# Graph layer on one core: layer 2 on split operands with 512 moving columns, its output turned back, and rings of six

## Chip, core and metric

One Trainium2 chip, one of its cores. The metric is the device time of one execution in microseconds; a comparison takes the median of several executions. The kernel before ran three times: 213.15 us median, 213.1 to 213.64.

## What is computed

`x` is 6250 nodes by 128, `edge_attr` is 106250 edges by 128, and `dst` (sorted) names the node of each edge. All in f32.

```python
h   = relu(layernorm(x))
agg = segment_sum(edge_attr, dst, 6250)          # [6250, 128]
hid = relu(concatenate([agg, h], axis=1) @ W1 + b1)   # W1 [256, 512]
out = x + hid @ W2 + b2                          # W2 [512, 128]
```

## The kernel before

Nodes are taken in NB = 25 blocks of 256 (the last has 106), edges in 69 full rounds of 1536 and a rest round. A round is one transfer of 768 KB into one slot of the ring `edges` (RING = 8 slots). VectorE (`build`, L474 to 486) compares the edges' relative node numbers with an iota and writes a one-hot matrix per round into a ring of HOTS = 8. TensorE (`sum_rounds`, L776) multiplies one-hot by edges, two, three or four rounds per block, into bank 0; ScalarE copies the sums out (`copy_sums`), TensorE turns them (`turn_sums`), and VectorE adds each piece of 32 nodes at its place in `aggT` (`add_sums`, L565), at addresses that `load_bases` reads into its registers.

Beside this runs the layer norm of block b: `stats` on VectorE, `spread` on Pool (four small instructions), `normalise` on ScalarE, `turn_x` on TensorE, `h_out` on ScalarE and `rest_of_h` on VectorE. The last two split the turned block in a high part `hT_hi` of type f32r and the rest `hT_lo`. `round_agg` and `rest_of_agg` do the same to the sums.

The network runs on groups: blocks 0, 1 and 2 alone, then pairs of blocks (3,4), (5,6) up to (23,24), so NS = 14 groups of which ten have 512 columns and the last 362. Layer 1 (`layer1_h` L828, `layer1_agg` L837) makes three f32r products for each of four parts t of 128 hidden units, the group's columns moving. `relu` on ScalarE (L409) writes `hidden` in f32, one instruction a part. `layer2` (L854) has `hidden` as weights and W2 as moving operand, in plain f32 with 128 moving columns: eight instructions for a single block, 16 for a pair. Its result has nodes on the partitions, so `finish` on VectorE adds it straight to `x`, to which `add_b2` (L507) has added b2, and SyncE stores it.

The order on each engine is written out by hand, as one loop over k = 1 to 24. Blocks up to k = 3 (EARLY) have an order of their own. From k = 5 on, an odd k holds layer 1 of a pair, the even k after it its layer 2:

```python
                    sum_rounds(k)
                    if k == EARLY + 1:
                        turn_x(k)
                    if two is not None:
                        layer2(two, two)
                    if one is not None:
                        layer1_h(one, one)
                    turn_sums(k)
                    if k + 1 < NB:
                        turn_x(k + 1)
                    if one is not None:
                        layer1_agg(one, one, blocks_of(one)[-1] + 1)
```

All loads and stores go out on SyncE's queue in order; `load(r)` waits until round r - RING has been summed. Semaphores are waited for in program order, so an instruction that waits holds all behind it on its engine.

## Time and profile before

| | us |
|---|---|
| median of three executions | 213.15 |
| the profiled execution, whole | 212.71 |
| its span in the trace | 210.5 |
| TensorE busy in the span | 193.7 |
| VectorE busy | 131.5 |
| ScalarE busy | 84.7 |
| Pool busy | 43.0 |

The profiled execution took 2.21 us more than its span (what lies outside the first and last instruction), and 0.44 us less than the median. Busy time of TensorE counts overlapping matmuls once. A plain f32 matmul shows as two records in the trace, so the 200 instructions of `layer2` are 400 records; an f32 transpose and an f32r matmul are one record each.

### The profile page before, as it was taken

Reading aid. Unit: us, or ns where it says so; the run is one execution under the profiler, and the core shown is the slowest. Engines: PE = TensorE matmul, PEld = TensorE weight load, DVE = VectorE, ACT = ScalarE, POOL = GpSimd, SP = SyncE. Lnnn points to the kernel's source line nnn. Section 1 sums busy time; section 2 is a strip of 40 time slices with the busy share of each in tenths; the row PEclk is TensorE's granted clock in tenths of the full one; section 3 lists DMA queues with packets and bytes.
Section 4 is the critical chain, followed back from the end, with each engine's and each line's share of the span. In section 5 each row is a group of like instructions: output and inputs, shape, how many; then the busy total and the mean of one; then the engine's idle time right before and its main releaser. Section 6 shows DMA issues by size and latency. Waiting matters only on the chain.

```text
span 210.5 us, 6775 instructions
## 1 busy us (share of the span) xinstructions
PE 193.7 (92%) x2549; PEld 164.9 (78%) x2549; DVE 131.5 (62%) x581; ACT 84.7 (40%) x185; POOL 43.0 (20%) x120
## 2 busy tenths in 40 slices
PE   1397999998999999999999999999999999999990
PEld 1165878788789888798898897887986987978990
DVE  1945754729766967786768579676774775853300
ACT  3031354272482363543713814734436236136030
POOL 5554020220222012202220221122022022200000
PEclk9999999999999999999999999999999999999997
DMA  6899999999999999999999999999999780010101
GB/s 213 272 391 361 377 371 377 376 375 385 386 377 384 377 376 387 377 380 384 365 350 372 328 381 376 311 299 386 306 379 378 226 320 36 3 50 3 50 15 30
DMA packets 44623, 62.55 MB, mean 297 GB/s; under 512 B 1795, under 2 KB 44294, under 8 KB 44588
## 3 DMA queue, kind: packets, MB, share of 16 engines
q1 hardware_dynamic: 44116, 61.66, 83.4%
q10 hardware_dynamic: 472, 0.43, 0.8%
q8 instruction: 22, 0.36, 0.7%
q14 instruction: 13, 0.11, 0.1%
HBM read 58.88 MB, written 3.20 MB: 295 GB/s over the span
## 4 chain that ended last, share of the span: by engine, by line
PE 79%; DMA 11%; SPq 3%; DVE 2%; ACT 1%; issue 1%; DVEq 0%; ACTq 0%
PE bank L854 21%; PE bank L793 20%; PE bank L828 16%; PE bank L837 15%; DMA edges<-in_edge_attr 6%; DMA xs<-in_x 5%; PE bank L804 3%; SPq L257 3%; PE bank L814 2%; PE bank L786 1%; ACT xn L378 1%; DVE aggT L576 1%; SPq L282 0%; ACT sums L393 0%; SPq L280 0%
## 5 line engine op out<-in xcount | busy, mean ns | idle before, releaser
L793 PE MATMUL bank<-edges,onehot 128*32 128x128 f32 x1656 | 55.1, 285 | 4.7 <-DMA edges<-in_edge_attr 3.9
L793 PEld LDWEIGHTS bank<-edges,onehot 128*32 128x32 f32 x1656 | 45.3, 114 | 12.5 <-issue 5.6
L854 PE MATMUL bank<-w,hidden 128*128 128x128 f32 (+1 forms) x400 | 48.5, 278 | 0.4 <-DVE outrow L552 0.4
L409 ACT ACTIVATE hidden<-bank,b_col 128x512 f32<-128x512 f32 (+2 forms) x56 | 34.2, 633 | 35.3 <-PE bank L837 35.3
L854 PEld LDWEIGHTS bank<-w,hidden 128*128 128x128 f32 (+1 forms) x400 | 45.8, 189 | 3.1 <-issue 2.2
L576 DVE TENSOR_TENSOR aggT<-bank,aggT 128x32 f32 x277 | 35.3, 190 | 17.0 <-issue 10.9
L378 ACT ACTIVATE xn<-xs,shift,rstd 128x128 f32<-128x128 f32 (+1 forms) x50 | 21.7, 484 | 44.4 <-POOL shift L334 44.2
L327 POOL TENSOR_SCALAR var<-meanvar 128x2 f32<-128x2 f32 (+1 forms) x25 | 7.3, 293 | 133.1 <-DVE meanvar L504 133.0
L484 DVE TENSOR_TENSOR onehot<-relT,iota 128x384 f32<-128x384 f32 x69 | 34.4, 552 | 0.0
L828 PE MATMUL bank<-hT_hi,w_hi 128*128 128x512 f32 (+2 forms) x56 | 22.5, 402 | 0.0
L837 PE MATMUL bank<-agg_hi,w_hi 128*128 128x512 f32 (+2 forms) x56 | 21.4, 382 | 0.3 <-DVE agg_lo L526 0.3
L828 PE MATMUL bank<-hT_lo,w_hi 128*128 128x512 f32 (+2 forms) x56 | 20.9, 372 | 0.0
L828 PE MATMUL bank<-hT_hi,w_lo 128*128 128x512 f32 (+2 forms) x56 | 20.7, 370 | 0.0
L837 PE MATMUL bank<-agg_hi,w_lo 128*128 128x512 f32 (+2 forms) x56 | 20.4, 364 | 0.0
L837 PE MATMUL bank<-agg_lo,w_hi 128*128 128x512 f32 (+2 forms) x56 | 20.3, 363 | 0.0
L332 POOL TENSOR_TENSOR rstd<-var,power 128x2 f32<-128x2 f32 (+1 forms) x25 | 17.7, 708 | 2.1
L399 ACT ACTIVATE agg_hi<-aggT 128x256 fp32r<-128x256 f32 (+1 forms) x25 | 10.7, 428 | 18.0 <-DVE aggT L576 17.9
L520 DVE TENSOR_TENSOR hT_lo<-bank,hT_hi 128x256 fp32r<-128x256 f32 (+1 forms) x25 | 10.3, 414 | 11.5 <-ACT hT_hi L385 11.4
L526 DVE TENSOR_TENSOR agg_lo<-aggT,agg_hi 128x256 fp32r<-128x256 f32 (+1 forms) x25 | 10.5, 419 | 8.8 <-ACT agg_hi L399 8.8
L499 DVE BATCH_NORM_STATS2 halves<-xs 128x6 f32<-128x128 f32 (+1 forms) x50 | 12.0, 281 | 5.5 <-DMA xs<-in_x 5.5
L393 ACT ACTIVATE sums<-bank 128x384 f32<-128x384 f32 (+3 forms) x25 | 11.7, 466 | 7.0 <-PE bank L793 6.1
L828 PEld LDWEIGHTS bank<-hT_hi,w_hi 128*128 128x128 f32 x56 | 10.9, 194 | 4.2 <-issue 2.8
(94 smaller groups left out, 170.8 us busy)
## 6 DMA issues: line engine op xcount, KB each, us to landing
edges<-in_edge_attr SPq DMA_DIRECT2D x69, 768.0 KB, 9.3
xs<-in_x SPq DMA_DIRECT2D x21, 128.0 KB, 9.3
out_rows<-outrow SPq DMA_DIRECT2D x10, 256.0 KB
w<-in_L_gnn_W SPq DMA_DIRECT2D x1, 512.0 KB, 9.7
out_rows<-outrow SPq DMA_DIRECT2D x4, 128.0 KB, 8.4
xs<-in_x SPq DMA_DIRECT2D x1, 256.0 KB, 11.4
w<-in_L_gnn_W SPq DMA_DIRECT2D x1, 256.0 KB, 12.8
hidden<-in_dst SPq DMA_DIRECT2D x1, 192.0 KB, 3.1
```

The source lines that it names most:

```text
L332: nc.gpsimd.tensor_tensor(rstd[0:w, par, :], var[0:w, par, :], power[0:w, :], ALU.pow).then_inc(pow_ready, 1)
L378: ins = nc.scalar.activation(xn[0:w, par, j, :], xs[0:w, b, j * F:(j + 1) * F], ACT.Relu, bias=shift[0:w, par, j:j + 1], scale=rstd[0:w, p ...
L393: nc.scalar.activation(sums[0:rows, k % 2, 0:n], sums_ps[0:rows, 0:n], ACT.Copy).then_inc(sums_copied, 1)
L399: nc.scalar.activation(agg_hi[:, halves].rearrange("f (j p) -> f j p", j=2), aggT[:, bass.ds(b * BLOCK, halves.stop - halves.start)].rearr ...
L409: nc.scalar.activation(hidden[:, t, 0:cols], hid_ps[t][:, 0:cols], ACT.Relu, bias=b1_col[:, t:t + 1]).then_inc(hidden_ready, 1)
L484: nc.vector.tensor_tensor(hot, of.unsqueeze(2).to_broadcast([p, n, W]), iota[0:p, 0:W].unsqueeze(1).to_broadcast([p, n, W]), ALU.is_equal) ...
L499: nc.vector.bn_stats(halves[0:w, par, j, :], xs[0:w, b, j * F:(j + 1) * F]).then_inc(halves_ready, 1)
L576: nc.vector.tensor_tensor(win, turn_ps[:, at:at + W], win, ALU.add).then_inc(agg_added, 1)
L793: ins = nc.tensor.matmul(sums_ps[t * W:(t + 1) * W, cols], onehot[:, hots, e, :], edges[:, slot, e * F:(e + 1) * F], start=(g == 0), stop= ...
L828: nc.tensor.matmul(hid_ps[t][:, 0:cols], wt[:, 1, to], v[:, here], start=(i == 0), stop=False)
L837: ins = nc.tensor.matmul(hid_ps[t][:, 0:cols], wt[:, 0, to], v[:, 0:cols], start=False, stop=(i == 2))
L854: ins = nc.tensor.matmul(o[0:w, j * F:(j + 1) * F], hidden[:, t, at:at + w], w2[:, t, :], start=(t == 0), stop=(t == HT - 1))
```

## The change

Layer 2 is turned round. Its weights are now the parts of W2, split as `w2_hi` and `w2_lo` of type f32r (made once, at k = 1: ScalarE L506, VectorE L761); the moving operand is the hidden part with all columns of the group, split as `hid_hi` and `hid_lo`. That is three f32r matmuls for each of four parts. The result has features on the partitions: ScalarE copies it out with b2 as bias (`out_copy`, L480), TensorE turns it back into the same bank (`turn_out`, L983), and `finish` reads that. `add_b2` is left only for the last two blocks; the last group keeps the old form (`layer2_last`).

To have `hid_lo`, ScalarE runs two instructions a part, one that writes the f32 value `full` (in the buffer of `w1`, two parts deep) and one that writes `hid_hi`. Pool subtracts for parts 0 and 1, VectorE for parts 2 and 3. ScalarE waits for `lo_by_pool` before it writes parts 2 and 3 into `full`. The rings of edges and one-hots have six slots. `dst` lands in the sixth edge slot, so the sixth load waits until `dst` has been read. The loads of `x` stand earlier in SyncE's order, and the stats, spread and normalise steps of two blocks stand together in every second k.

```diff
-RING = 8
-HOTS = 8
+RING = 6
+HOTS = 6
@@ Pool
-            for b in range(1, NB):
-                spread(b)
+            def rest_of_hidden(n, s):
+                cols = cols_of(s)
+                for t in range(HALF):
+                    pool.wait_ge(hidden_ready, n * HT + t + 1)
+                    nc.gpsimd.tensor_tensor(hid_lo[:, t, 0:cols], full[:, t % 2, 0:cols],
+                                            hid_hi[:, t, 0:cols].bitcast(F32), ALU.subtract).then_inc(lo_by_pool, 1)
...
+            for k in range(EARLY + 2, NB, 2):
+                for b in (k + 3, k + 4):
+                    if b < NB:
+                        spread(b)
+                rest_of_hidden(group1(k), group1(k))
@@ ScalarE, relu and what is new
-                    nc.scalar.activation(hidden[:, t, 0:cols], hid_ps[t][:, 0:cols], ACT.Relu,
-                                         bias=b1_col[:, t:t + 1]).then_inc(hidden_ready, 1)
+                    if t >= HALF:
+                        act.wait_ge(lo_by_pool, split_before(n) * HALF + t - HALF + 1)
+                    elif not (isinstance(n, int) and n == 0):
+                        act.wait_ge(lo_by_dve, (split_before(n) - 1) * HALF + t + 1)
+                    nc.scalar.activation(full[:, t % 2, 0:cols], hid_ps[t][:, 0:cols], ACT.Relu, bias=bias_col[:, t:t + 1])
+                    nc.scalar.activation(hid_hi[:, t, 0:cols], hid_ps[t][:, 0:cols], ACT.Relu,
+                                         bias=bias_col[:, t:t + 1]).then_inc(hidden_ready, 1)
+
+            def out_copy(n, s):
+                cols = cols_of(s)
+                act.wait_ge(out_summed, n + 1)
+                nc.scalar.activation(outT[:, 0:cols], out_ps[:, 0:cols], ACT.Identity,
+                                     bias=bias_col[:, HT:HT + 1]).then_inc(outT_ready, 1)
@@ VectorE
+            def rest_of_hidden(n, s, t):
+                cols = cols_of(s)
+                dve.wait_ge(hidden_ready, n * HT + t + 1)
+                nc.vector.tensor_tensor(hid_lo[:, t, 0:cols], full[:, t % 2, 0:cols], hid_hi[:, t, 0:cols].bitcast(F32),
+                                        ALU.subtract).then_inc(lo_by_dve, 1)
@@ TensorE
+            def layer2(n, s, first=0, last=HT):
...
+                for t in range(first, last):
+                    if t < HALF:
+                        pe.wait_ge(lo_by_pool, split_before(n) * HALF + t + 1)
+                    else:
+                        pe.wait_ge(lo_by_dve, split_before(n) * HALF + t - HALF + 1)
+                    products = ((w2_hi, hid_hi), (w2_hi, hid_lo), (w2_lo, hid_hi))
+                    for i, (wt, v) in enumerate(products):
+                        ins = nc.tensor.matmul(out_ps[:, 0:cols], wt[:, t, :], v[:, t, 0:cols], start=(t == 0 and i == 0),
+                                               stop=(t == HT - 1 and i == 2))
...
+            def turn_out(n, s):
+                pe.wait_ge(outT_ready, split_before(n) + 1)
+                for j in range(cols_of(s) // P):
+                    ins = nc.tensor.transpose(out_ps[:, j * F:(j + 1) * F], outT[:, j * P:(j + 1) * P], ident[:, :])
+                ins.then_inc(out_turned, 1)
@@ TensorE, the loop from k = 4 on
+                elif one is not None:
+                    sum_rounds(k)
+                    turn_out(group3(k), group3(k))
+                    layer1_h(one, one)
+                    turn_sums(k)
+                    if k + 1 < NB:
+                        turn_x(k + 1)
+                    layer1_agg(one, one, blocks_of(one)[-1] + 1)
                 else:
                     sum_rounds(k)
...
+                    layer2(two, two, 0, 3)
                     turn_sums(k)
+                    layer2(two, two, 3)
                     if k + 1 < NB:
                         turn_x(k + 1)
```

How the instructions now stand, in rows of the program's order. First TensorE at k = 6 and the start of k = 7 (`bank` is a PSUM bank, `w` and `hidden` are W2 and the hidden units). Before:

```order
L793 MATMUL bank<-edges,onehot 32x128 x36
L854 MATMUL bank<-w,hidden 128x128 x16
L804 MATMUL bank<-ident,sums 128x128 x3
L814 MATMUL bank<-ident,xn 128x128 x2
L793 MATMUL bank<-edges,onehot 32x128 x36
L828 MATMUL bank<-hT_hi,w_hi 128x512
```

After, from the last of the first three parts on:

```order
L975 MATMUL bank<-hid_hi,w_hi 128x512
L975 MATMUL bank<-hid_lo,w_hi 128x512
L975 MATMUL bank<-hid_hi,w_lo 128x512
L928 MATMUL bank<-ident,sums 128x128 x3
L975 MATMUL bank<-hid_hi,w_hi 128x512
L975 MATMUL bank<-hid_lo,w_hi 128x512
L975 MATMUL bank<-hid_hi,w_lo 128x512
L938 MATMUL bank<-ident,xn 128x128 x2
L917 MATMUL bank<-edges,onehot 32x128 x36
L983 MATMUL bank<-ident,outT 128x128 x4
L952 MATMUL bank<-hT_hi,w_hi 128x512
```

Sixteen instructions have become twelve with four times the columns, turning the sums (L928) stands between the third and the fourth part, and four transposes (L983) stand ahead of the next layer 1.

Second ScalarE at k = 1, behind the first group's sums. Before:

```order
L399 ACTIVATE agg_hi<-aggT 128x256
L409 ACTIVATE hidden<-bank,b_col 128x256 x4
L378 ACTIVATE xn<-xs,shift,rstd 128x128 x2
L393 ACTIVATE sums<-bank 128x384
L378 ACTIVATE xn<-xs,shift,rstd 128x128 x2
L385 ACTIVATE hT_hi<-bank 128x256
```

After, from the last of four pairs of relu instructions on (`w` at L473 is `full`, in the buffer of w1; at L506 it is W2):

```order
L473 ACTIVATE w<-bank,bias_col 128x256
L474 ACTIVATE hid_hi<-bank,bias_col 128x256
L506 ACTIVATE w_hi<-w 128x512
L434 ACTIVATE xn<-xs,shift,rstd 128x128 x2
L449 ACTIVATE sums<-bank 128x384
L434 ACTIVATE xn<-xs,shift,rstd 128x128 x2
L441 ACTIVATE hT_hi<-bank 128x256
```

Eight relu instructions and the rounding of W2 now stand ahead of the normalising of block 1 and of the copy of the sums, where four relu instructions stood.

## Rows read from the trace of the kernel before

**Rows 1.** The page: busy tenths in 40 slices of 5.26 us.

```profile
PE   1397999998999999999999999999999999999990
DMA  6899999999999999999999999999999780010101
```

**Rows 2.** The chain that ended last: start us, us, what; two stretches.

```profile
56.55 3.02 PE bank L837 x12
...
169.15 2.10 PE bank L793 x72
171.25 3.00 PE bank L828 x12
174.25 0.33 PE bank L804 x3
174.57 0.22 PE bank L814 x2
174.79 2.77 PE bank L837 x12
177.56 1.45 PE bank L793 x48
179.01 3.77 PE bank L854 x32
```

**Rows 3.** ScalarE and VectorE by line and form: count, busy us, mean ns, idle before.

```profile
L409 ACT ACTIVATE hidden<-bank,b_col 128x512 f32<-128x512 f32 x40 | 27.4, 688 | 27.0 <-PE bank L837 26.9
L484 DVE TENSOR_TENSOR onehot<-relT,iota 128x384 f32<-128x384 f32 x69 | 34.4, 552 | 0.0
L554 DVE TENSOR_TENSOR outrow<-bank,xs 128x512 f32<-128x512 f32 x10 | 6.9, 692 | 10.8 <-DMA out_rows<-outrow 4.6 <-issue 2.5 <-PE bank L854 2.4
```

**Rows 4.** Timeline of ScalarE: start us, us, instruction; relu of block 0, then of a pair.

```profile
24.94 1.57 ACT L409 ACTIVATE hidden<-bank,b_col 128x256 f32<-128x256 f32 x4 [1.45 <-PE bank L837]
26.38 0.89 ACT L378 ACTIVATE xn<-xs,shift,rstd 128x128 f32<-128x128 f32 x2
...
175.53 2.76 ACT L409 ACTIVATE hidden<-bank,b_col 128x512 f32<-128x512 f32 x4 [2.95 <-PE bank L837]
178.19 0.87 ACT L378 ACTIVATE xn<-xs,shift,rstd 128x128 f32<-128x128 f32 x2
```

**Rows 5.** Timeline of TensorE, 27 to 46 us, with the idle time before.

```profile
27.34 0.44 PE L814 MATMUL bank<-ident,xn 128*128 128x128 f32 x2
...
29.30 2.05 PE L854 MATMUL bank<-w,hidden 128*128 128x128 f32 x16
...
36.59 0.55 PE L804 MATMUL bank<-ident,sums 128*128 128x128 f32 x3 [0.24 <-ACT sums L393]
...
45.58 0.55 PE L804 MATMUL bank<-ident,sums 128*128 128x128 f32 x3 [0.24 <-ACT sums L393]
```

**Rows 6.** Timelines of VectorE and ScalarE, 43 to 48 us.

```profile
43.38 0.25 DVE L504 BATCH_NORM_AGGREGATE meanvar<-halves 128x2 f32<-128x6 f32 x2
...
45.43 1.64 ACT L378 ACTIVATE xn<-xs,shift,rstd 128x128 f32<-128x128 f32 x4
...
47.36 0.42 DVE L520 TENSOR_TENSOR hT_lo<-bank,hT_hi 128x256 fp32r<-128x256 f32 x1 [2.50 <-ACT hT_hi L385]
```

**Rows 7.** Pool by line and form: count, busy us, mean ns, idle before.

```profile
L350 POOL MEMSET aggT<- 128x832 f32 x8 | 6.0, 791 | 1.4 <-DVE relA L581 1.4
L334 POOL TENSOR_TENSOR shift<-negmean,rstd 128x2 f32<-128x2 f32 x24 | 4.7, 195 | 1.9
```

**Rows 8.** Timelines of Pool and VectorE: L327 of block 1 and of a later block.

```profile
18.35 0.22 POOL L327 TENSOR_SCALAR var<-meanvar 128x2 f32<-128x2 f32 x1 [4.48 <-DVE meanvar L504]
...
101.65 0.30 POOL L327 TENSOR_SCALAR var<-meanvar 128x2 f32<-128x2 f32 x1 [5.72 <-DVE meanvar L504]
...
101.48 0.39 DVE L513 TENSOR_TENSOR xs<-xs,b_all 128x256 f32<-128x256 f32 x1
```

**Rows 9.** The page: DMA issues, count, KB each, median us to landing.

```profile
edges<-in_edge_attr SPq DMA_DIRECT2D x69, 768.0 KB, 9.3
```

More of the change, by code:

```diff
@@ L298, in _ @@
                         load(r + RING)
[L299 to L300 removed]
+                if not early and group3(k - 1) is not None:
+                    store(group3(k - 1), group3(k - 1))
             store(NS - 2, NS - 2)
@@ L439, in _ @@
                     copy_sums(k)
                     normalise(k + 1)
-                if k == EARLY:
-                    normalise(k + 2)
-                if not early and k + 2 < NB:
-                    normalise(k + 2)
+                    if k == EARLY:
+                        normalise(k + 2)
+                elif one is not None:
+                    h_out(k)
+                    copy_sums(k)
+                    round_agg(k - 1, chunks_by(k - 1), place(k - 1), group_of(k - 1))
+                    if k + 1 < NB:
+                        h_out(k + 1)
+                    relu(one, one)
+                else:
+                    if k == EARLY + 1:
+                        h_out(k - 1)
+                    copy_sums(k)
+                    if k == EARLY + 1:
+                        h_out(k)
+                    round_agg(k - 1, chunks_by(k - 1), place(k - 1), group_of(k - 1))
+                    out_copy(two, two)
+                    for b in (k + 2, k + 3):
+                        if b < NB:
+                            normalise(b)
@@ L457, in again_group @@
                     relu(n, s)
+                    if not (isinstance(s, int) and s == NS - 1):
+                        out_copy(n, s)
                 for s in range(ONES):
@@ L653, in _ @@
                         build(r)
-                rest_of_agg(k - 1, k - 1, place(k - 1))
+                if k == EARLY + 1 or (k > EARLY and one is None):
+                    rest_of_h(k)
+                if k <= EARLY:
+                    rest_of_agg(k - 1, k - 1, place(k - 1))
                 if k + 1 < NB:
@@ L698, in _ @@
                     nc.vector.tensor_scalar(flag[:, :], colD[:, 6:7], 0.0, None, ALU.is_gt).then_inc(flag_ready, 1)
+                if k > EARLY and one is None:
+                    rest_of_agg(k - 1, k - 1, place(k - 1))
                 bases = load_bases(k)
-                if group2(k) is not None:
-                    finish(group2(k), group2(k))
+                if k <= EARLY and group3(k) is not None:
+                    finish(group3(k), group3(k))
             add_sums(NB - 1, bases)
             rest_of_agg(NB - 1, NB - 1, place(NB - 1))
+            finish(NS - 2, NS - 2)
+            add_b2(NB - 2)
             add_b2(NB - 1)
```

206 lines of the change are left out of this document (138 added, 68 removed).

## The prediction

> **What bounds the kernel now.** I read the page's slices first, then the chain, then the timelines of the engines that feed TensorE. The slices show TensorE at nine tenths nearly throughout, and a DMA that is as full until slice 31 and then falls off while TensorE goes on [rows 1]. So the transfers finish early, and the end is set by TensorE. The chain says the same: from 56.55 us on it is TensorE's own instructions one behind the other, with no idle piece between them [rows 2]. There every microsecond taken from or added to TensorE's stream counts in full, and so does every wait. Before that the chain passes through other engines: TensorE waits for sums and layer norms that ScalarE and VectorE hand over [rows 5, 6]. The question is thus what twelve wide products save on TensorE, and whether ScalarE, Pool and VectorE deliver split hidden parts in time.
>
> **TensorE's own work.** A pair of blocks (odd k, then even k) costs, by the chain, 2.10 + 3.00 + 0.33 + 0.22 + 2.77 for the odd k and 2.10 + 3.77 + 0.33 + 0.22 for the even one, 14.84 us together; three of the ten even k have two rounds, 1.45 in place of 2.10 [rows 2]. Layer 2 is the 3.77. The new one has twelve f32r products with 512 moving columns, like layer 1. Nine come behind the rounds, as L828 does (9/12 of 3.00, 2.25), three behind transposes, as L837 (3/12 of 2.77, 0.69). Four f32 transposes at 0.11 each (0.33 for three, [rows 2]) are 0.44, and splitting the products around the turning of the sums gives one more change of kind, about 0.1 (the 3.00 against the 2.77 shows what one costs, at most 0.23). The sum is 3.48 against 3.77: **0.29 less a pair, 2.9 less for ten**. The bounds are 0.1 and 0.5 a pair. The last group is unchanged. Single blocks gain some 0.3 each, which is in the steps below.
>
> **The start, k = 1 to 5.** One relu of 256 columns takes a pitch of 0.36 (26.38 less 24.94, over four [rows 4]), and there are now eight. At k = 1 relu starts at 24.94 as before and ends at 27.8; rounding W2 (512 columns, one pitch of a pair's relu, 0.59) ends at 28.4; only then block 1 is normalised, 0.8, to 29.2. TensorE wanted it at 27.34 [rows 5]. The sums are copied behind it in some 0.5 (384 columns, between the pitches 0.36 for 256 and 0.59 for 512) and turned at 29.7; before, with both done in time, the turning was 0.7 behind L814's 27.34, so it is 1.7 late. At k = 2 layer 2 costs 1.5 in place of 2.05 [rows 5], so layer 1 ends 1.1 late; relu then holds ScalarE for 2.9 and not 1.4, the copy of the sums stands behind it, and the turning at 36.59 goes to 38.6. At k = 3 the same: layer 2 waits a little for `finish` of block 0, which on VectorE now stands behind two subtractions, and 45.58 becomes 48.05, 2.5 late. At k = 4 there is a second chain. VectorE takes the stats of block 5 behind the subtractions of group 2, so they end at 48.75, not at 43.63; Pool needs 1.75 for the spread (before, from 43.63 to the normalising at 45.43 [rows 6]), ScalarE 0.8 for block 5's normalising and 0.35 for `h_out`, so VectorE's `rest_of_h` (47.36, [rows 6]) starts at 51.7, 4.3 late. At k = 5 VectorE has also the subtraction of `finish` and the stats of block 7 ahead of what layer 1 of the first pair needs, and I get that start at 61.3 where the chain has 56.55 [rows 2]: **4.8 more**. Bounds: 2, if only the first delay stays, and 6.5.
>
> **A pair's hidden parts.** Let A be the start of `layer1_agg` in the chain, 174.79. Relu starts at 175.53, A + 0.74 [rows 2, 4]. Its four instructions last 2.76, each 0.69 [rows 3], so the last starts at 177.60, and the next instruction at 178.19: a pitch of 0.59 where nothing is waited for. Parts 0 to 3 are then high at A + 2.0, 3.2, 4.4 and 5.6. TensorE reaches parts 0 and 2 at A + 4.87 and A + 6.4, the turning of the sums at A + 7.1 and part 3 at A + 7.45; all 0.65 earlier with two rounds. VectorE's subtraction of 512 columns I take at 0.69, as L554 [rows 3]: part 3 is ready at A + 6.3. That would be 1.1 in hand, but Pool lies between: relu may not begin part 2 before Pool's part 0 is done. Pool's subtraction is not in the trace. Below, it lies at 0.49 + 0.2: one stream of 832 columns takes 0.79 [rows 7], so 512 take 0.49, and the same kind on two columns takes 0.195. Above, three streams of 0.49 and 0.2, 1.7. I take two streams, as its two inputs seem the nearer count to a write-only memset: **1.2 us**. (The Trainium skill, GPSIMD Engine Reference, section 3.1, has 2.6 cycles an element for this kind at 1.2 GHz, which makes 1.1; no run here has yet shown it.) Pool also has two spreads of 1.45 to 1.75 ahead of it, whose stats VectorE ends near A. So its part 0 ends about A + 3.8, part 1 at 5.0, and relu's part 3 is high at 6.2, its rest ready at 7.0, still in hand by 0.4 with three rounds, and late by 0.2 with two.
>
> Then VectorE. It loses one `add_b2` a block (0.39) and gains two subtractions a pair (1.3), so it is about 0.5 busier, and in the first pair, still late from the start, its stats come so late that Pool begins part 0 at about A + 5: TensorE waits 0.9 there. VectorE builds one-hots (0.55, [rows 3]) just while Pool works. Pool's L327 on the same two columns takes 0.22 at block 1 and 0.30 at a later block, where VectorE's two-input L513 runs until 0.22 after its start [rows 8]; the two may hold each other up. (The Trainium skill, SBUF — State Buffer, section "SBUF: two separate sides", calls their shared port pair an exclusive lock against two-input VectorE instructions; the 0.08 agrees, and is all the trace has of it.) For what a few such meetings and the pairs with two rounds cost I take 0.25 for each of nine pairs, 2.2; below it is 0, above it is 1.2, one whole Pool instruction.
>
> **Ring and loads.** With six slots a load is issued when the round six before it is summed, two blocks ahead, some 13 us, and lands 9.3 after issue [rows 9]. I cost it at nothing; if that cover went, TensorE would wait for edges. Moving b2 into `out_copy`, the extra small load, the earlier loads of x and the later sixth load stand beside other work: nothing. `out_copy` and `turn_out` have the rounds of the next k between them.
>
> **Sum.** 4.8 - 2.9 + 0.9 + 2.2 = 5.0 us more. The profiled execution had 212.71, the median 213.15; on the median that is **218.2**, and I say 218.0.
>
> **Rivals.**
> - *ScalarE and Pool stay covered and the start heals.* TensorE's idle at the start is partly made up, since VectorE's and Pool's queues are shorter than I reckon and x comes earlier; no pair waits. From the point where the start costs less than 2.6 us the change is faster. With a start at +1 it is 213.15 - 2.9 + 1 = 211.3. For it: the hidden parts are in hand by 0.4 on paper. Against: the first 1.7 at k = 1 follows from ScalarE's order alone. 0.14.
> - *Pool and VectorE block each other in every pair.* If one-hots wait for a Pool subtraction and Pool for one-hots, part 3 comes about 1 us late ten times: 213.15 + 4.8 - 2.9 + 10 = 225.2. For it: the 0.30 against 0.22, and the rule of the page named above, which by the same working gives this 225. Against: 0.08 is little. 0.2.
> - *The ring starves.* If transfers bunch and land 15 us after issue, TensorE waits about 1.5 a pair: 213.15 + 2 + 15, some 230. Against: TensorE takes its 4.98 MB a pair more slowly than the DMA has brought them so far. 0.04.
> - *Forecast*, 213.3 to 222, 0.62.
>
> **The numbers.** Differences under 0.3% (0.64 us) can't be told here. Faster: the first rival, less its near part, 0.12. Same: its edge and the forecast's lower edge, 0.05. Slower: 0.83. The range takes the lower bounds of start and waits (213.15 + 2 - 2.9 + 1 = 213.3) and upward most of the second rival: 213.3 to 224.0; what is left out is most of the first rival and the upper part of the second and third.
>
> **What would show it.** Right: L975 and L983 together about 3.4 a pair on TensorE; TensorE idle at L938 near 29 us, and at the turning of the sums at k = 2 and 3 for ScalarE; the first pair's `layer1_agg` (L961) near 61; Pool's L389 near 1.2; waits at L975 for VectorE's rest. Wrong: a first pair near 57, or Pool's L389 stretched beyond 1.7, or TensorE waiting for edges.

## The result and the profile after

| | before | after |
|---|---|---|
| median of four executions, us | 213.39 | 229.69 |
| lowest to highest | 213.1 to 214.07 | 228.85 to 231.23 |
| the profiled execution, whole | 212.71 | 231.23 |
| its span | 210.5 | 229.4 |

The change makes the kernel slower by 7.9% (ratio 1.079, interval 1.075 to 1.084). The forecast was 218.0, range 213.3 to 224.0: the sign is right, the size is not (16.3 us more, not 5). The profiled execution is the slowest of its four, so the pieces below add up to its own 18.9 us of span; 1.5 us of them lie between it and the median. Here and below, medians and ratios leave out executions in the chip's slower state, in which the granted clock is lower and the time over 1.5% above the kernel's fastest.

The page of the changed kernel, first the busy times, then the slices (5.74 us each) and the chain by engine and by line:

```profile
PE 196.4 (86%) x2383; PEld 155.2 (68%) x2383; DVE 149.7 (65%) x587; ACT 117.7 (51%) x251; POOL 73.4 (32%) x146
...
PE   1498688775999998989999779989999879999990
...
PEclk9999979999799999999999999999999999999998
DMA  6899999897897989989969979989799499200011
...
PE 40%; DMA 23%; DVE 20%; issue 6%; ACT 4%; SPq 2%; POOL 2%; DVEq 1%; ACTq 0%; POOLq 0%
DMA out_rows<-outrow 19%; PE bank L917 11%; PE bank L961 9%; PE bank L952 7%; DVE onehot L571 7%; PE bank L975 6%; DMA edges<-in_edge_attr 4%; DVE aggT L671 3%; DVE halves L586 2%; PE bank L998 2%; SPq L282 2%; DVE outrow L643 2%; ACT hid_hi L474 1%; DVE hid_lo L650 1%; PE bank L928 1%
```

Two things stand out beside [rows 1]. TensorE has holes from slice 4 to 10, the start, and then again and again to the end. And the chain, which was TensorE's own [rows 2], now lies for 19% in a **store**: `out_rows<-outrow`. No term of the prediction had a store in it.

The starts of `layer1_agg` (L837 before, L961 after) cut the span into stretches that can be compared. They are the first record of that line for the group:

| | first pair (3,4) | tenth pair (21,22) | the nine steps between | from there to the end |
|---|---|---|---|---|
| before | 56.52 | 188.83 | 132.31 | 21.7 |
| after | 65.08 | 207.75 | 142.67 | 21.7 |
| difference | +8.6 | | +10.4 | 0.0 |

The start was predicted at +4.8 and the pairs at 0.9 + 2.2 less 2.9, about nothing. So the start took almost twice what was forecast, and the pairs took ten microseconds that the forecast did not have.

**Where TensorE waits.** The waits of the changed kernel, those of TensorE alone (total us, times, longest us):

```profile
PE bank L975 <- DVE hid_lo L650: 4.5, 7, 1.6
...
PE bank L928 <- ACT sums L449: 3.4, 3, 1.3
PE bank L975 <- POOL hid_lo L389: 2.7, 6, 0.6
PE bank L961 <- DVE agg_lo L612: 2.5, 3, 1.4
PE bank L938 <- DVE hT_lo L606: 2.2, 1, 2.2
PE bank L938 <- ACT xn L434: 2.2, 1, 2.2
PE bank L975 <- DVE outrow L641: 0.6, 1, 0.6
```

The rows for `hid_lo` are the pairs', and so is 1.9 of the 2.5 us for `agg_lo` (9.1 us together); the others are the start's. The idle time that a row shows is less than what is lost, since ends of matmuls are modelled. One pair shows it. Timeline of TensorE in the changed kernel, layer 2 of the pair (7,8), from the last product of its first part to the start of its third:

```profile
101.75 0.40 PE L975 MATMUL bank<-hid_hi,w_lo 128*128 128x512 f32 x1
102.67 0.50 PE L975 MATMUL bank<-hid_hi,w_hi 128*128 128x512 f32 x1 [0.52 <-POOL hid_lo L389]
103.01 0.40 PE L975 MATMUL bank<-hid_lo,w_hi 128*128 128x512 f32 x1
103.24 0.40 PE L975 MATMUL bank<-hid_hi,w_lo 128*128 128x512 f32 x1
104.15 0.50 PE L975 MATMUL bank<-hid_hi,w_hi 128*128 128x512 f32 x1 [0.51 <-DVE hid_lo L650]
```

Products that follow one another start 0.23 us apart (103.01 to 103.24). Across the wait the starts are 0.92 apart, so 0.69 is lost where the row says 0.52. With TensorE's saving of 0.39 a pair (measured below), the nine steps hold 10.4 + 3.5, some 14 us of waits.

**The store.** Timeline of the changed kernel around the pair (9,10), SyncE first, then VectorE, TensorE and Pool:

```profile
115.89 2.31 SPq L282 DMA_DIRECT2D edges<-in_edge_attr  x3
118.25 0.51 SPq L300 DMA_DIRECT2D out_rows<-outrow  x1
...
109.24 0.68 DVE L643 TENSOR_TENSOR outrow<-bank,xs 128x512 f32<-128x512 f32 x1
...
123.86 0.42 DVE L606 TENSOR_TENSOR hT_lo<-bank,hT_hi 128x256 fp32r<-128x256 f32 x1
127.24 0.69 DVE L643 TENSOR_TENSOR outrow<-bank,xs 128x512 f32<-128x512 f32 x1 [2.96 <-DMA out_rows<-outrow]
127.84 0.42 DVE L612 TENSOR_TENSOR agg_lo<-aggT,agg_hi 128x256 fp32r<-128x256 f32 x1
...
128.31 0.50 PE L961 MATMUL bank<-agg_hi,w_hi 128*128 128x512 f32 x1 [1.35 <-DVE agg_lo L612]
...
129.09 0.22 POOL L354 TENSOR_SCALAR var<-meanvar 128x2 f32<-128x2 f32 x1 [11.90 <-DVE meanvar L591]
```

And the chain of waits there (start us, us, what):

```profile
117.70 0.50 SPq L282
118.25 8.90 DMA out_rows<-outrow
127.24 0.69 DVE outrow L643
...
128.31 3.06 PE bank L961 x12
```

`finish` (L643) writes `outrow` at 109.24. The store of it stands on SyncE behind the loads of the even k, which wait for their slots, so it is issued only at 118.25, 8.3 us after `finish` ended, and is done 8.9 us later. The next `finish` was ready to go at 124.28 and waits 2.96 for it, since for pairs there is one `outrow`. Behind it in VectorE's queue stand `agg_lo`, for which TensorE waits, and the stats of two blocks, for which Pool waits, which has then its spreads ahead of its subtractions. In the kernel before the order was another: `finish` stood at the end of the even k, behind `agg_lo` and the stats. Its store stood behind the loads of the odd k that follows at once, and in the corresponding place it was issued 1.8 us after `finish` ended (111.37 to 113.13). `finish` waited for stores there too, 4.6 us in all [rows 3], but no wait of TensorE in the pairs came of it.

**Pool and VectorE hold each other up.** By line and form, the changed kernel (count, busy us, mean ns, idle before):

```profile
L571 DVE TENSOR_TENSOR onehot<-relT,iota 128x384 f32<-128x384 f32 x69 | 45.2, 706 | 0.0
...
L389 POOL TENSOR_TENSOR hid_lo<-w,hid_hi 128x512 fp32r<-128x512 f32 x20 | 27.6, 1402 | 12.8 <-ACT hid_hi L474 12.8
...
L643 DVE TENSOR_TENSOR outrow<-bank,xs 128x512 f32<-128x512 f32 x10 | 6.9, 691 | 11.3 <-DMA out_rows<-outrow 7.8 <-PE bank L983 2.0 <-issue 1.6
```

The same one-hot instruction took 552 ns before [rows 3] and now takes 706 on average (544 to 1645). Timelines of Pool and VectorE in one pair:

```profile
99.77 2.84 POOL L389 TENSOR_TENSOR hid_lo<-w,hid_hi 128x512 fp32r<-128x512 f32 x2
...
100.65 2.85 DVE L571 TENSOR_TENSOR onehot<-relT,iota 128x384 f32<-128x384 f32 x3
```

Three one-hots, 1.49 us when alone (at 99.33 in the kernel before), take 2.85 beside Pool's two subtractions. VectorE's own subtractions stand behind them.

**The start.** Timeline of TensorE in the changed kernel: its longest waits from k = 1 to 4, and the two rounds that follow:

```profile
29.52 0.69 PE L938 MATMUL bank<-ident,xn 128*128 128x128 f32 x2 [2.17 <-ACT xn L434]
...
40.78 0.55 PE L928 MATMUL bank<-ident,sums 128*128 128x128 f32 x3 [1.34 <-ACT sums L449]
...
50.91 0.55 PE L928 MATMUL bank<-ident,sums 128*128 128x128 f32 x3 [1.34 <-ACT sums L449]
...
55.14 0.41 PE L938 MATMUL bank<-ident,xn 128*128 128x128 f32 x2 [2.24 <-DVE hT_lo L606]
...
58.68 2.92 PE L917 MATMUL bank<-edges,onehot 128*32 128x128 f32 x72
```

The places are the ones forecast. The first turning of the sums is nearly where it was reckoned (30.0 against 29.7), the next two are later: 40.78 and 50.91 against 38.6 and 48.05. The last row is a loss of another kind: 72 records that take 2.17 at full clock (experiment 12) take 2.92, in one of the two slices where the page's granted clock falls to 7 tenths; the other holds the wait at 29.52. Windows of this trace put the granted clock at 0.51 from 30.0 to 33.0 and at 0.50 from 57.0 to 60.0, about the lower of its two levels (1.2 of 2.4 GHz). Six microseconds at half the clock are about 3 us of delay (an estimate from these windows), and the kernel before has no such slice.

### The profile page after: what moved, and what is told of

Read it like the earlier page. It is cut to its first block, busy times and chain, and to the rows that moved or that the text cites. A ratio compares the mean times of both kernels' runs of the same rounds, so it can differ in the third digit from the quotient of the medians.

```text
span 229.4 us, 6586 instructions
## 1 busy us (share of the span) xinstructions
PE 196.4 (86%) x2383; PEld 155.2 (68%) x2383; DVE 149.7 (65%) x587; ACT 117.7 (51%) x251; POOL 73.4 (32%) x146
## 4 chain that ended last, share of the span: by engine, by line
PE 40%; DMA 23%; DVE 20%; issue 6%; ACT 4%; SPq 2%; POOL 2%; DVEq 1%; ACTq 0%; POOLq 0%
DMA out_rows<-outrow 19%; PE bank L917 11%; PE bank L961 9%; PE bank L952 7%; DVE onehot L571 7%; PE bank L975 6%; DMA edges<-in_edge_attr 4%; DVE aggT L671 3%; DVE halves L586 2%; PE bank L998 2%; SPq L282 2%; DVE outrow L643 2%; ACT hid_hi L474 1%; DVE hid_lo L650 1%; PE bank L928 1%
## 5 line engine op out<-in xcount | busy, mean ns | idle before, releaser
L473 ACT ACTIVATE w<-bank,bias_col 128x512 f32<-128x512 f32 (+1 forms) x52 | 33.3, 640 | 24.0 <-POOL hid_lo L389 12.2
L571 DVE TENSOR_TENSOR onehot<-relT,iota 128x384 f32<-128x384 f32 x69 | 45.2, 706 | 0.0
L389 POOL TENSOR_TENSOR hid_lo<-w,hid_hi 128x512 fp32r<-128x512 f32 (+1 forms) x26 | 32.0, 1247 | 28.4 <-ACT hid_hi L474 28.4
L474 ACT ACTIVATE hid_hi<-bank,bias_col 128x512 fp32r<-128x512 f32 (+1 forms) x52 | 33.1, 636 | 0.0
L975 PE MATMUL bank<-hid_hi,w_hi 128*128 128x512 f32 (+1 forms) x52 | 23.2, 447 | 8.1 <-DVE hid_lo L650 4.5
L441 ACT ACTIVATE hT_hi<-bank 128x256 fp32r<-128x256 f32 (+1 forms) x25 | 9.3, 371 | 31.8 <-PE bank L938 31.8
L650 DVE TENSOR_TENSOR hid_lo<-w,hid_hi 128x512 fp32r<-128x512 f32 (+1 forms) x26 | 15.5, 622 | 14.5 <-ACT hid_hi L474 14.5
L961 PE MATMUL bank<-agg_hi,w_hi 128*128 128x512 f32 (+2 forms) x56 | 21.6, 385 | 2.5 <-DVE agg_lo L612 2.5
L975 PEld LDWEIGHTS bank<-hid_hi,w_hi 128*128 128x128 f32 x52 | 10.1, 193 | 17.1 <-DVE hid_lo L650 8.6
L961 PE MATMUL bank<-agg_hi,w_lo 128*128 128x512 f32 (+2 forms) x56 | 20.4, 364 | 0.0
L961 PE MATMUL bank<-agg_lo,w_hi 128*128 128x512 f32 (+2 forms) x56 | 20.4, 364 | 0.0
L975 PE MATMUL bank<-hid_lo,w_hi 128*128 128x512 f32 (+1 forms) x52 | 19.4, 372 | 0.0
L975 PE MATMUL bank<-hid_hi,w_lo 128*128 128x512 f32 (+1 forms) x52 | 19.3, 372 | 0.0
```

The lines of the kernel that those rows point to most:

```text
L389: nc.gpsimd.tensor_tensor(hid_lo[:, t, 0:cols], full[:, t % 2, 0:cols], hid_hi[:, t, 0:cols].bitcast(F32), ALU.subtract).then_inc(lo_by_po ...
L473: nc.scalar.activation(full[:, t % 2, 0:cols], hid_ps[t][:, 0:cols], ACT.Relu, bias=bias_col[:, t:t + 1])
L474: nc.scalar.activation(hid_hi[:, t, 0:cols], hid_ps[t][:, 0:cols], ACT.Relu, bias=bias_col[:, t:t + 1]).then_inc(hidden_ready, 1)
L571: nc.vector.tensor_tensor(hot, of.unsqueeze(2).to_broadcast([p, n, W]), iota[0:p, 0:W].unsqueeze(1).to_broadcast([p, n, W]), ALU.is_equal) ...
L650: nc.vector.tensor_tensor(hid_lo[:, t, 0:cols], full[:, t % 2, 0:cols], hid_hi[:, t, 0:cols].bitcast(F32), ALU.subtract).then_inc(lo_by_dv ...
L961: ins = nc.tensor.matmul(hid_ps[t][:, 0:cols], wt[:, 0, to], v[:, 0:cols], start=False, stop=(i == 2))
```

## Experiments

The theory after reading: of the 16 us, the store wait ahead of `agg_lo` and the stats costs the most in the pairs, the mutual blocking the next, and the start is ScalarE's and VectorE's order. The rival: the rests are late because Pool and ScalarE are simply too slow for a pair (12.2 us of ScalarE's waits for Pool), so that order changes little. Each ratio is to the kernel before on the same chip. The chips differ: the kernel before has medians from 212.49 to 213.39 on them, so a difference between two experiments is good to about 1 us.

**1. Rings of six in the kernel before.**

```diff
-RING = 8
-HOTS = 8
+RING = 6
+HOTS = 6
```

> The kernel before with both rings cut from eight to six slots and nothing else. Theory W (the loss comes from waits in the chain relu, rests, store and finish): 213.4 us as before, within 0.6, TensorE waits for edges only at the start. Rival R (the smaller ring starves TensorE): most of the 16 us, at least 217.

Measured: 213.11 us, ratio 1.000 (0.998 to 1.002). The smaller rings cost nothing in the order of before, as the prediction had it; in the new order the ring of eight was not run.

**2. `finish` behind `agg_lo` and the stats** (odd k, VectorE).

```diff
-                    finish(group3(k), group3(k))
                     rest_of_agg(k - 1, k - 1, place(k - 1))
                     for b in (k + 3, k + 4):
                         if b < NB:
                             stats(b)
+                    finish(group3(k), group3(k))
```

> The changed kernel, but at odd k VectorE rounds off the sums (agg_lo) and takes the stats before it does finish. Theory S (finish waits for the store of the group before, 8.5 us after its issue, and holds all behind it on VectorE): VectorE still waits at finish, but TensorE no longer waits at layer1_agg, and Pool's spreads and its first subtraction come earlier in the pairs where ScalarE waited 2 us; 222 to 226 us. Rival (the store wait is mostly beside TensorE's work, which shows only 2 us idle at layer1_agg): 227 to 228.

Measured: 223.88 us, ratio 1.052 (1.049 to 1.055), 5.8 less than the change. `finish` itself now waits less as well; the row by form of this kernel:

```profile
L643 DVE TENSOR_TENSOR outrow<-bank,xs 128x512 f32<-128x512 f32 x10 | 6.8, 680 | 4.1 <-DMA out_rows<-outrow 2.8 <-PE bank L983 1.3
```

TensorE has no row left that waits for Pool's `hid_lo`, though nothing of Pool's work was changed: Pool had been late because the stats ahead of its spreads were. The move takes two things out of the way, the wait for the store and the instruction itself (0.69). Over the nine steps of the profiled executions it gives 6.9 us, of which 2.7 lie in steps where `finish` had waited 0.2 or less for a store. How the gain divides between the two is not shown by this run; 4 and 5 show it without the subtractions.

**3. One-hots behind VectorE's subtractions** (even k from 6 on), so that Pool and VectorE do not read side by side.

```diff
-                if k + 1 < NB:
+                late = k > EARLY + 1 and one is None
+                if k + 1 < NB and not late:
                     for r in ROUNDS[k + 1]:
                         build(r)
...
                         rest_of_hidden(group2(k), group2(k), 2)
                         rest_of_hidden(group2(k), group2(k), 3)
+                if k + 1 < NB and late:
+                    for r in ROUNDS[k + 1]:
+                        build(r)
```

> The changed kernel, but at even k from 6 on VectorE builds the next one-hots after its two subtractions, so they no longer run beside Pool's. Theory L (a Pool subtraction and a two-input VectorE instruction hold each other up): Pool's subtraction of 512 columns falls from 1.40 to 1.2 us or less, the one-hots from 0.71 to 0.55, and the time to about 225. Rival (Pool just takes 1.4 us, and one-hots are late for another reason): both durations stay and the time is within 1 us of 229.7, or longer, since the one-hots come later.

Measured: 227.66 us, ratio 1.069 (1.067 to 1.072), 2.0 less than the change. By form:

```profile
L571 DVE TENSOR_TENSOR onehot<-relT,iota 128x384 f32<-128x384 f32 x69 | 34.4, 551 | 0.0
...
L389 POOL TENSOR_TENSOR hid_lo<-w,hid_hi 128x512 fp32r<-128x512 f32 x20 | 25.2, 1282 | 11.7 <-ACT hid_hi L474 11.6
```

Both are back at a length of their own: the one-hot at 551 ns (552 before), Pool's subtraction at 1.28, a little above the 1.2 expected. So they do hold each other up. The gain is 2 us, less than the 4.7 expected and far from the 10 of the second rival; it is a net figure, since the one-hots now also come later.

**4. No rests at all.** `hid_lo` is a constant, nobody subtracts, and ScalarE runs one instruction a part.

```diff
-                    nc.scalar.activation(full[:, t % 2, 0:cols], hid_ps[t][:, 0:cols], ACT.Relu, bias=bias_col[:, t:t + 1])
...
-                for t in range(HALF):
+                for t in range(0):
                     pool.wait_ge(hidden_ready, n * HT + t + 1)
...
             def rest_of_hidden(n, s, t):
-                cols = cols_of(s)
-                dve.wait_ge(hidden_ready, n * HT + t + 1)
...
+                return
```

> The changed kernel without the rest of the hidden part: ScalarE writes only the high part (one instruction a part), hid_lo is filled once with a constant and read as before, Pool and VectorE subtract nothing. TensorE's instructions are the same. Left out: the correction of the hidden part's rounding. If TensorE's own saving is 0.29 us a pair and the loss is all in making the rests: 210 to 213 us. If the new order or the wide products cost TensorE by themselves: 215 or more.

Measured: 213.76 and 216.0 us (and 219.96 and 220.53 at a granted clock of 0.98), too far apart for a ratio. The profiled one (216.0, span 214.1) starts its first pair at 55.50, a little earlier than before does, and is slower than before all the same. By the expectation's numbers that would mean that the new order or the wide products cost TensorE something; the rows show that it is the order, by way of the store. The row for `finish` by form, two of its instructions in VectorE's timeline, and the row of TensorE's waits:

```profile
L640 DVE TENSOR_TENSOR outrow<-bank,xs 128x512 f32<-128x512 f32 x10 | 6.9, 692 | 24.0 <-DMA out_rows<-outrow 22.0 <-PE bank L974 2.0
```

```profile
70.84 0.69 DVE L640 TENSOR_TENSOR outrow<-bank,xs 128x512 f32<-128x512 f32 x1 [3.94 <-DMA out_rows<-outrow]
...
99.84 0.69 DVE L640 TENSOR_TENSOR outrow<-bank,xs 128x512 f32<-128x512 f32 x1 [1.06 <-DMA out_rows<-outrow]
```

```profile
PE bank L955 <- DVE agg_lo L609: 7.1, 6, 2.0
```

With every rest gone, VectorE stands 22.0 us before the stores and TensorE 7.1 us behind it. A VectorE with less to do only comes to the store earlier.

**5. No rests, and `finish` late** (4 and 2 together): what the change gives TensorE when nothing else is late.

```diff
-                    finish(group3(k), group3(k))
                     rest_of_agg(k - 1, k - 1, place(k - 1))
...
+                    finish(group3(k), group3(k))
```

> No rests are made (as in a_no_rest; left out is the correction of the hidden part's rounding), and finish stands behind agg_lo. Nothing but the start should then hold TensorE up, so it shows what TensorE's new instructions save alone. Theory: 0.29 a pair less than before, the pair 14.55 us from layer1_agg to layer1_agg where before has 14.82, and 209 to 211 us in all. Rival (the new instructions save nothing): pair at 14.8 and time at 213.

Measured: 207.09 us, ratio 0.975 (0.973 to 0.976). Over the nine steps the profiled execution is 8.6 us shorter than that of 4 (128.67 against 137.29).

Step by step, 4 and 5 separate the store wait from the instruction. In 4 `finish` stands ahead of `agg_lo` in every pair. Where it waits 1.06 or 0.66 us for a store, or not at all, the step is as long as in 5: the instruction in front costs nothing there. Where it waits 2.63 to 4.19, six times, the step is longer than in 5 by 0.69 to 2.28, each time by the wait less 1.9. So the whole 8.6 us are store waits, each beyond what lay covered. In 5 `finish` still waits 9.2 us for stores, and no pair is longer for it.

A pair of three rounds each takes 14.43 from one `layer1_agg` to the next, against 14.82 to 14.84 before (the first 14.44 and 14.88). TensorE's saving is thus **0.39 to 0.40 a pair**; the prediction had 0.29, within bounds of 0.1 and 0.5. Ten pairs make 4.0 of the 5.4 us; nearly all the rest, 1.3, is the single blocks', since the first pair starts at 55.19 and not at 56.52.

**6. Both moves with the rests in place** (2 and 3).

```diff
-                    finish(group3(k), group3(k))
                     rest_of_agg(k - 1, k - 1, place(k - 1))
...
+                    finish(group3(k), group3(k))
...
+                if k + 1 < NB and late:
+                    for r in ROUNDS[k + 1]:
+                        build(r)
```

> Both edits together: finish behind agg_lo and the stats at odd k, one-hots behind the two subtractions at even k. If store wait and blocking are two causes, their gains (5.8 and 2.0 us in the first four runs) add up to about 222; if they are one wait seen twice, it stays at 223.9.

Measured: 222.48 us, ratio 1.045 (1.042 to 1.049). Behind `finish` late, the later one-hots give 1.4 where they gave 2.0 alone. The two gains nearly add up, as for two causes; whether the missing 0.6 had been the same time can't be told, since the interval of each ratio is about 0.7 us to either side.

**7. The start in another order, on top of 6.** ScalarE at k = 1 rounds W2 and normalises block 1 ahead of the relu; for k up to 3 it copies the sums between relu parts 1 and 2; VectorE takes the stats, `w2_lo` and `finish` ahead of its subtractions; Pool spreads block 5 ahead of the rests of group 2.

```diff
@@ ScalarE
                 if k <= EARLY:
+                    if k == 1:
+                        act.wait_ge(w2_landed, 16)
+                        nc.scalar.activation(w2_hi[:, :, :], w2[:, :, :], ACT.Copy).then_inc(w2_hi_ready, 1)
+                        normalise(1)
...
-                    relu(one, one)
...
+                    relu(one, one, 0, HALF)
                     copy_sums(k)
+                    relu(one, one, HALF, HT)
@@ VectorE
                 if k <= EARLY:
-                    rest_of_hidden(one, one, 2)
-                    rest_of_hidden(one, one, 3)
                     stats(k + 2)
...
+                    if group3(k) is not None:
+                        finish(group3(k), group3(k))
+                    rest_of_hidden(one, one, 2)
+                    rest_of_hidden(one, one, 3)
```

> a_both_late, and the start reordered: at k = 1 ScalarE rounds W2 and normalises block 1 ahead of relu; at k = 1 to 3 it copies the sums between parts 1 and 2 of relu; VectorE takes the stats and finish ahead of its two subtractions; Pool's spread of block 5 stands ahead of group 2's. If the start's 8.6 us are these four orders, the first pair's layer1_agg comes at 58 to 60 instead of 65, and the time is 5 to 7 us under a_both_late. If the start is lost to the added work whatever its order, less than 2 us.

Measured: 217.63 us, ratio 1.026 (1.023 to 1.030), 4.9 less than 6 on the same chip (4.1 by the ratios). The first pair starts at 58.53, where 6 has 63.96. The largest wait left is at k = 4, for block 4's rest on VectorE; and in every pair ScalarE still waits for Pool. Timelines of TensorE and of ScalarE:

```profile
50.09 0.41 PE L943 MATMUL bank<-ident,xn 128*128 128x128 f32 x2 [2.97 <-DVE hT_lo L607]
...
108.96 0.69 ACT L473 ACTIVATE w<-bank,bias_col 128x512 f32<-128x512 f32 x1 [1.36 <-POOL hid_lo L389]
```

**8. All four subtractions on VectorE**, `finish` late, Pool free.

```diff
@@ Pool
-                for t in range(HALF):
+                for t in range(0):
@@ VectorE, rest_of_hidden(n, s, t)
+                first = 0 if t == 2 else 3
+                for u in range(first, t + 1):
+                    dve.wait_ge(hidden_ready, n * HT + u + 1)
+                    nc.vector.tensor_tensor(hid_lo[:, u, 0:cols], full[:, u % 2, 0:cols],
+                                            hid_hi[:, u, 0:cols].bitcast(F32),
+                                            ALU.subtract).then_inc(lo_by_dve if u >= HALF else lo_by_pool, 1)
```

> a_finish_late with all four subtractions on VectorE, Pool only spreads. No Pool instruction can block VectorE, but VectorE has 1.4 us more a pair, and relu's part 2 waits for VectorE's part 0, behind sums and one-hots. If blocking outweighs the work: under 223.9. If VectorE's added work counts: 226 or more.

Measured: 234.41 us, ratio 1.104 (1.102 to 1.107), some 11 more than with Pool (2). Waits of this kernel:

```profile
ACT w L473 <- DVE hid_lo L652: 25.4, 9, 6.2
...
PE bank L978 <- DVE hid_lo L652: 14.7, 17, 3.6
```

A VectorE subtraction takes 0.69 where Pool's takes 1.28, and still the kernel is slower: on VectorE the first parts stand behind one-hots and sums, and ScalarE waits up to 6.2 us for a free `full`. In this order Pool as a second engine is worth having; another order for the four subtractions on VectorE was not tried.

**9. Pool's rests between its two spreads**, on top of 7.

```diff
-                for b in (k + 3, k + 4):
-                    if b < NB:
-                        spread(b)
+                if k + 3 < NB:
+                    spread(k + 3)
                 rest_of_hidden(group1(k), group1(k))
+                if k + 4 < NB:
+                    spread(k + 4)
```

> a_late_early, and Pool makes the rests of a pair between the two spreads and not behind both. In a_late_early ScalarE waits 1.4 us in each pair for Pool's part 0, which starts 3.4 us after layer1_agg, 1.1 after its input is there. If that is what holds the pairs at 15.1 us on average (14.4 without rests), relu's wait falls to about 0.3, the pairs to about 14.6, and the time to 213 or less. If the pairs are held by ScalarE's eight instructions themselves, the time stays within 1 us of 217.6.

Measured: 213.15 us, ratio 1.003 (1.001 to 1.005), 4.5 less than 7 (5.0 by the ratios). The pairs of three rounds take 14.4 to 14.6, the pace of experiment 5. ScalarE's waits for Pool fall from 12.2 us in the changed kernel to 4.1. That answers the rival: with all subtractions made, Pool and ScalarE are fast enough for this pace once the order lets them start in time.

**10. The same Pool order in the changed kernel alone.** The diff is that of 9.

> The changed kernel with one edit: Pool makes a pair's rests between its two spreads. Behind the other edits this was worth 4.5 us. If the order on Pool is a cause by itself: 3 to 5 us less, 225 to 226.5. If the store wait and the blocking hide it: less than 1.5 us.

Measured: 228.55 us (227.98 to 230.48), ratio 1.075 (1.068 to 1.082). By itself the move that gave 4.5 us gives about 1, and the interval overlaps that of the change (1.075 to 1.084). ScalarE's waits for Pool do fall, from 12.2 to 4.1 us as in 9, but `finish` waits 11.9 us for its stores where it waited 7.8: the earlier Pool brings VectorE to the store earlier.

**11. k = 3 rearranged, on top of 9.** ScalarE runs `h_out(3)` and `normalise(4)` ahead of relu parts 2 and 3, VectorE `rest_of_h(3)` ahead of its subtractions.

```diff
@@ ScalarE
                     copy_sums(k)
+                    if k == EARLY:
+                        h_out(k)
+                        normalise(k + 1)
                     relu(one, one, HALF, HT)
-                    normalise(k + 1)
+                    if k != EARLY:
+                        normalise(k + 1)
@@ VectorE
+                    if k == EARLY:
+                        rest_of_h(k)
                     rest_of_hidden(one, one, 2)
```

> c_pool_mid, and at k = 3 ScalarE takes h_out of block 3 and the normalising of block 4 ahead of relu's parts 2 and 3, with VectorE's rest of it ahead of its subtractions; at k = 4 they held TensorE up for 3.0 us. Expected: that wait under 0.7 us, the first pair's layer1_agg at 56 to 57, and 2 us under c_pool_mid: 211, below the kernel before.

Measured: 212.62 us, ratio 0.998 (0.995 to 1.001), not the 211 expected: the 3 us wait is gone, and less than 1 us of it has come back. In the profiled execution the first pair starts at 59.42, not at 56 to 57. Timeline of TensorE, and a window over the rounds behind it (length, busy time of PE, PEld, DVE, ACT and POOL, granted clock, DMA share, GB/s):

```profile
51.19 0.41 PE L938 MATMUL bank<-ident,sums 128*128 128x128 f32 x2 [2.37 <-DVE aggT L675]
...
52.10 3.84 PE L927 MATMUL bank<-edges,onehot 128*32 128x128 f32 x72
```

```profile
52.00:54.00 2.00, 2.00 (x41) 1.90 (x43) 1.73 (x7) 1.23 (x3) 0.31 (x2) 0.55 1.07 399
```

The wait has moved to the sums, 2.37 us, and behind it the clock is granted at 0.55, about the lower of the two levels (1.2 of 2.4 GHz): 72 records take 3.84 in place of 2.17. Executions with a mean granted clock of 0.993 and more took 210.7 to 211.3, those near 0.987 took 212.4 to 213.4.

**12. The bases of k = 3 read ahead of the subtractions, on top of 11.** `add_sums` of k = 3 gets its addresses while TensorE works.

```diff
                         rest_of_h(k)
+                        bases = load_bases(k)
                     rest_of_hidden(one, one, 2)
...
-                bases = load_bases(k)
+                if k != EARLY:
+                    bases = load_bases(k)
```

> c_best, and at k = 3 VectorE reads the next addresses ahead of its two subtractions and not behind them. In c_best TensorE waits 2.4 us at k = 4 for add_sums of block 3, and the 36 products behind that wait take 3.8 us in place of 2.2. If the wait gets 0.6 shorter and the slow stretch behind it is set off by its length: 210.5 to 211, and the same in all runs. If only the wait itself counts: 212.0, and the runs stay spread between 210.7 and 213.4.

Measured: **210.48 us** (210.02 to 210.72), ratio 0.986 (0.984 to 0.989): 1.4% faster than the kernel before. Page and timeline of TensorE:

```profile
PE 191.5 (92%) x2383; PEld 154.4 (74%) x2383; DVE 139.2 (67%) x587; ACT 118.0 (57%) x251; POOL 75.1 (36%) x146
...
PE   1397999997999999999999999999998999999990
```

```profile
50.12 0.41 PE L940 MATMUL bank<-ident,sums 128*128 128x128 f32 x2 [1.54 <-DVE aggT L675]
...
51.03 2.17 PE L929 MATMUL bank<-edges,onehot 128*32 128x128 f32 x72
```

From the third slice to the last but one TensorE is at nine tenths again, but for two sevens and an eight. The first pair starts at 56.67, within 0.2 of before, and the nine steps take 130.40 against 132.31. The four executions lie within 0.7 us, where the twelve of experiment 11 spread over 2.7.

## Why the forecast had the sign and not the size

- **TensorE's own work: right.** 0.39 to 0.40 a pair against 0.29, within its bounds (experiment 5). So was the reading of the chain, but for half a microsecond at 162.15, where VectorE's `over` (L693) stands between TensorE's pieces.
- **The start: the step with the right mechanism and a size too small.** The text had ScalarE's eight relu instructions and VectorE's subtractions ahead of what TensorE wants, and named where it shows; all these waits are there. It took 8.6 and not 4.8, above the upper bound of 6.5. The turnings of the sums come 0.3, 2.2 and 2.9 us later than reckoned. What the sum didn't have is the clock, which fell behind the waits at 29.52 and 55.14: about 3 us by the estimate above, of the 3.8 that are missing. No run has these waits without the fall, so the share is not shown more closely. With the order of 7, 11 and 12 the start is as early as before (56.67), with the same work in it: order, not load, made the 8.6.
- **Pool's subtraction: right in size.** 1.28 us alone and 1.40 in company, against 1.2 with bounds 0.69 and 1.7. The Trainium skill, GPSIMD Engine Reference, section 3.1, gives 2.6 cycles an element, an estimate of 1.1 us for 512; the rows are above it. 256 columns took 0.73 at the shortest, so 512 are not twice that: about 0.18 lies in each instruction whatever its size, and Pool's smallest ones [rows 7] take as much.
- **"a few such meetings ... I take 0.25 for each of nine pairs": this is the term that failed.** It was the only one for waits in the pairs after the first. Together with the 0.9 it had 3.1 us, and the nine steps hold about 14. It looked for them in the one place, Pool's and VectorE's mutual blocking, which the experiments put at 2.0 (3) or 1.4 (6). The larger pieces, the order around `finish` (2) and Pool's order (9), were not in the sum.
- **The step that was missing: `finish` on VectorE.** "`out_copy` and `turn_out` have the rounds of the next k between them" is right, and was as far as the text went. The step moved on VectorE too, from behind `agg_lo` and the stats to ahead of them, and with it the wait for the previous store; the store moved on SyncE's queue from behind the loads of the odd k to behind those of the even k. Neither queue was costed for it. [rows 3] had the warning: 4.6 us of VectorE's idle time before L554 was for `out_rows`. That wait had been free because of what stood behind it, not because it was short. Experiments 4 and 5 show it without any rest in play, step by step. With the rests, the move gave 5.8 us (2).
- **Pool's order: half right.** Part 0 was to be done at about 3.8 behind the start of `layer1_agg`; in the pair at 112.02 the two subtractions run from 114.35 to 117.19, so part 0 ends near 3.8 and part 1 at 5.2. But "still in hand by 0.4" left no room for the slower one-hots, and both spreads ahead of the subtractions turned out worth 4.5 us once the rest was mended (9), about 1 before (10). The text had this order and found the part in hand on paper; over the nine steps it cost 5.2, the second piece of the 14.
- **The rivals.** The first (start heals, pairs covered, 211.3) is what experiment 12 reaches with 210.5, but only with the orders changed. The second (its sum is 225.05, not the 225.2 of the text) has a reason that carries only 2 of the 16 us. The third, a starving ring, has the measured size (some 230) by luck: it is ruled out by 1 for the order of before, and in the changed kernel TensorE's waits for edges sum to 3.8 in three places, as in experiment 12.
- **Rings of six at nothing: right** (1), for the order of before. The other small edits, put at nothing too, were not run by themselves.

The two stretches of each profiled execution show where each edit acts:

| | first pair | nine steps |
|---|---|---|
| before | 56.52 | 132.31 |
| the change | 65.08 | 142.67 |
| 3, one-hots late | 64.41 | 140.52 |
| 2, `finish` late | 64.58 | 135.82 |
| 6, both | 63.96 | 135.34 |
| 7, and the start | 58.53 | 135.44 |
| 9, and Pool's order | 59.03 | 130.25 |
| 12, and k = 3 | 56.67 | 130.40 |
| 5, no rests, `finish` late | 55.19 | 128.67 |

The pairs' loss is thus first the order around `finish` (6.9 us) and then Pool's order (5.2 us), and the mutual blocking is 0.5 once `finish` is late.

From the change down to the best kernel the steps are, in the order tried, 5.8 (`finish`), 1.4 (one-hots), 4.9 (start), 4.5 (Pool), 0.5 and 2.1 (k = 3): 19.2 us (by the ratios 5.8, 1.3, 4.1, 5.0, 1.1 and 2.4). They don't stand for independent costs. The same Pool move is worth about 1 first and 4.5 last, so a list in another order would share them out otherwise.

Not tried: a second `outrow`, or the store ahead of the loads, which would take the store wait away at its root; an iota in another memory, to see whether the one-hots then still hold Pool up; the ring of eight in the new order. What a pair still loses against experiment 5, 1.7 us over nine steps in experiment 12, was not taken apart.

## What to carry to other kernels

When a step is moved on an engine, list every wait inside it and what now stands behind it; a wait in a profile that costs nothing is a property of its place, and it comes due when something urgent is put behind it. A store's completion counts from its issue, so look where it stands in its queue: here 8.3 us of queue came before 8.9 of transfer. And try an order change again after the others: behind another wait it can measure next to nothing.

## What the runs showed of the hardware

- **Pool and VectorE hold each other up.** One-hot instructions with two inputs went from 552 to 706 ns on average, the longest 1645, while Pool's subtraction took 1402 on average, the longest 1675, and 1282 when kept apart; keeping them apart in time removed all of it on both. (The Trainium skill, SBUF — State Buffer, section "SBUF: two separate sides", has this as a lock between the two; the numbers agree in kind.) What was not expected is how little it costs in the end: 10.8 us more VectorE time for one-hots made 2.0 us of kernel time, and 1.4 behind a late `finish`.
- **The clock after a pause.** In the changed kernel the granted clock fell to about 0.5 after idle times of 2.17 and 2.24 us, in experiment 11 after 2.37 (0.55 granted); in experiment 9 it stayed up after 2.95 (72 records at 53.38 took 2.17), in 7 after 2.97, and in 12 after 1.54. So the length of the pause alone does not tell it. What else does was not separated by these runs. In experiment 11 the executions of one kernel lie some 2 us apart, with their mean granted clock.
- **A store of 256 KB** issued among loads of 768 KB took 8.2 to 8.9 us to be done, in the five places where the chain of the changed kernel shows it.
